# Cross-attention and experts on one core: two vectors loaded as rows, the first query's high products first, x statistics spread over the first pairs

## The reference

```python
# x (16,128,256); ctx_1024 (16,128,256); norm_w, gate_b (256,)
def xattn(h, mem):
    normed = rmsnorm(h, eps=1e-6) * norm_w
    v_pool = concat([normed, mem], axis=1)          # 256 rows per batch
    q = normed @ q_w.T;  k = v_pool @ k_w.T
    attn = softmax(where(mask, q @ k.T / 16, -inf)) # causal on the first 128, all of mem
    h_tilde = attn @ v_pool
    alpha = sigmoid(h @ gate_w.T + gate_b)
    return (1 - alpha) * h + alpha * h_tilde
x = x + xattn(layernorm(x), ctx_1024)
x = x + experts(layernorm(x), combine_weights, top_idx, W1, b1, W2, b2)   # 8 experts, 512 tokens each
```

## Time and profile before

| | us |
|---|---|
| median of 3 runs (lowest, highest) | 274.97 (274.80, 275.33) |
| the profiled execution, whole time | 275.01 |
| the profiled execution, span | 273.2 |

### The profile page before, as it was taken

One profiled execution on the slowest core, in us unless ns is written; L12 is line 12 of the kernel. 1 busy time (PEld: TensorE's weight loads), 2 busy tenths in 40 slices (PEclk: granted clock), 3 DMA queues, 4 the chain that ended last, 5 costly groups with the idle time before them and its releaser, 6 DMA issues.

```text
span 273.2 us, 5127 instructions
## 1 busy us (share of the span) xinstructions
PE 263.7 (97%) x1477; PEld 225.8 (83%) x1477; DVE 218.4 (80%) x553; ACT 188.2 (69%) x349; POOL 156.9 (57%) x152
## 2 busy tenths in 40 slices
PE   7899999999989999999999999999999999999993
PEld 3688899999876888888888888888888888888983
DVE  1899999899985779968878896796887889689453
ACT  2687899887666975786676587668657758773540
POOL 4349765565768717656456466655645656514525
PEclk9999999999999999999999999999999999999998
DMA  5986257588446945454464544645446561210211
GB/s 154 341 232 199 94 154 200 148 231 270 133 149 150 388 154 157 129 169 155 134 208 154 156 142 135 168 118 207 160 138 180 160 181 56 59 35 34 65 49 69
DMA packets 30560, 42.44 MB, mean 155 GB/s; under 512 B 5521, under 2 KB 24283, under 8 KB 30416
## 3 DMA queue, kind: packets, MB, share of 16 engines
q1 hardware_dynamic: 25120, 29.74, 35.0%
q0 software_dynamic: 4608, 12.24, 15.4%
q10 hardware_dynamic: 816, 0.26, 0.4%
HBM read 33.54 MB, written 9.24 MB: 157 GB/s over the span
## 4 chain that ended last, share of the span: by engine, by line
PE 81%; DVE 6%; issue 4%; DMA 4%; POOL 1%; ACT 1%; SPq 0%; DVEq 0%; POOLq 0%
PE bank L1423 19%; PE bank L1202 12%; PE bank L1203 12%; PE bank L1204 12%; PE bank L1424 10%; PE bank L1250 4%; PE bank L1294 3%; DMA x_all<-in_x_dram 2%; PE bank L1351 2%; DMA x_all<-token_rows,idx_all 2%; PE bank L1370 1%; PE bank L1371 1%; PE bank L1374 1%; PE bank L1318 1%; POOL out_dram L557 1%
## 5 line engine op out<-in xcount | busy, mean ns | idle before, releaser
L752 ACT ACTIVATE keysT<-bank,biasT 128x512 f32<-128x512 f32 x63 | 43.6, 692 | 55.6 <-PE bank L1204 39.3
L557 POOL DMA_INDIRECT out_dram<-h,sidx x32 | 36.7, 1146 | 40.2 <-DVE h L1094 34.8
L547 POOL DMA_INDIRECT x_all<-out_dram,idx_all x32 | 36.6, 1143 | 23.6 <-DMA out_dram<-h,sidx 16.0
L1202 PE MATMUL bank<-x_hi,w_parts 128*128 128x512 f32 (+1 forms) x114 | 45.1, 396 | 0.0
L1203 PE MATMUL bank<-x_lo,w_parts 128*128 128x512 f32 (+1 forms) x114 | 44.4, 389 | 0.0
L1204 PE MATMUL bank<-x_hi,w_parts 128*128 128x512 f32 (+1 forms) x114 | 44.1, 387 | 0.0
L1119 DVE TENSOR_TENSOR g_lo<-keysT,g_hi 128x512 fp32r<-128x512 f32 x32 | 22.1, 692 | 27.0 <-ACT g_hi L753 26.3
L543 POOL DMA_INDIRECT x_all<-token_rows,idx_all x28 | 30.7, 1095 | 18.9 <-DVE factor L1143 12.4
L1423 PE MATMUL bank<-w_parts,g_hi 128*128 128x512 f32 x112 | 40.5, 396 | 0.0
L1124 DVE TENSOR_TENSOR w_parts<-w_raw,w_parts 128x512 fp32r<-128x512 f32 x56 | 38.4, 686 | 0.0
L758 ACT CAST w_parts<-w_raw 128x512 fp32r<-128x512 f32 x56 | 34.9, 623 | 0.0
(11 more groups left out here) (187 smaller groups left out, 681.5 us busy)
## 6 DMA issues: line engine op xcount, KB each, us to landing
w_raw<-in_L_ffn_W_dram SPq DMA_DIRECT2D x32, 512.0 KB
idx_rows<-in_L_ffn_top_idx_dram SPq DMA_DIRECT2D x8, 256.0 KB, 4.1
out_dram<-x SPq DMA_DIRECT2D x8, 256.0 KB, 2.9
hn_cnat<-in_ctx_dram SPq DMA_DIRECT2D x7, 256.0 KB, 2.8
token_rows<-xn SPq DMA_DIRECT2D x7, 256.0 KB, 2.2
hn_cnat<-in_L_ffn_b_dram SPq DMA_DIRECT2D x1, 1024.0 KB
x_all<-in_x_dram SPq DMA_DIRECT2D x3, 256.0 KB, 6.8
x_all<-in_x_dram SPq DMA_DIRECT2D x1, 768.0 KB, 9.4
```

What stands on the lines that cost most here:

```text
L547: g.indirect_dma_start(accg[:, t, :], None, flat, list_of(e, t)).then_inc(acc_in[t], 16)
L557: g.indirect_dma_start(flat, idx(sidx[:, t:t + 1].bitcast(U32), 0), newrow[:, t, :], None, bounds_check=N - 1, oob_is_err=False).then_inc( ...
L752: a.activation(g32[:, f % NG, :], ps_up[f % 2][:, :], ACT.Gelu_apprx_tanh, bias=bias)
L1202: t_.matmul(dst, lhs_hi, rhs_hi, start=first, stop=False)
```

## The change

- **Vectors.** norm_w and gate_b are loaded as two rows into one partition (`vec_row`), still from ScalarE's queue behind k_w. Between `M_rows(0)` and `M_rows(1)` TensorE makes four products of a 128-wide piece of the row with a 1x1 tile `one` (set by GpSimd) and so puts the pieces in four columns of bank 6; ScalarE copies these to `norm_w_gate_bT`. All that needed norm_w by partition waits for that copy.
- **TensorE.** Eight warming products, not ten. The four spreading transposes come before hn's of pair 0. In the first query each half's four products with hnT's high part come first and its two with the low part last, and only these wait for the low part. `hn_transposes(2)` moves from before pair 0's values product to behind the list's transposes.
- **SP.** `load_ctx(0)` and `load_x(1)` change places.
- **ScalarE.** `vec_bc` is copied behind query(0) and gateT's high part; hn of pair 1 goes to VectorE; `hn_transposed(1)` moves between the two exponentials of pair 0; `hn_transposed(2)` and `normed_transposed(2)` move to the end of pair 0's body.
- **VectorE.** `x_sums` of batch 2 moves behind `hnT_low(0)`; hn of pair 1 and gateT's low part come before both masks of pair 0, h of pair 0 and `x_rms(0, 4)` behind them; statistics in groups 6-7 and 8-9 (pair 0), 10-13 (pair 1), 14-15 (pair 2), with `x_rms` for 4-9 in pair 1 and 10-15 in pair 4; the casts of lists go behind the gate logit of pair 0; `hnT_low(2)` moves to pair 1's body, where the variance of x2 also comes ahead of `hnT_low(3)`. All bodies are written out, with no loop.
- **GpSimd.** Powers and shifts follow the smaller groups, in pairs 0 to 3.

```diff
-            act.dma_start(norm_wT, norm_w.rearrange("(k p) -> p k", p=P), allow_slow_non_contiguous=True)\
-                .then_inc(nwT_in, 16)
-            act.dma_start(norm_w_gate_bT[:, 1, :], gate_b.rearrange("(k p) -> p k", p=P),
-                          allow_slow_non_contiguous=True).then_inc(gate_b_in, 16)
+            act.dma_start(vec_row[:, 0:H], norm_w.rearrange("(a h) -> a h", a=1)).then_inc(vec_in, 16)
+            act.dma_start(vec_row[:, H:2 * H], gate_b.rearrange("(a h) -> a h", a=1)).then_inc(vec_in, 16)
...
+            act.wait_ge(cols_mm, 1)
+            a.copy(norm_w_gate_bT[:, :, :].rearrange("p n k -> p (n k)"), ps_cols).then_inc(cols_rdy, 1)
...
+                    if is_first(p) and b == 0:
+                        hn_transposed(1, 1)
...
             hn_rows(0, 0)
-            x_sums(2, 3, 1)
-            dve.wait_ge(nwT_in, 16)
+            dve.wait_ge(cols_rdy, 1)
             M_low(0)
             M_low(1)
             hnT_low(0, 0)
-            x_sums(3, 4, 1)
+            x_sums(2, 4, 1)
             x_aggregates(2, 4)
             x_variances(2, 4)
             x_stats(4, 6, 2)
             x_variances(4, 6)
-            h_rows(0, 0, False)
-            x_rms(0, 4, 2)
-            x_sums(6, 8, 3)
...
+                else:
+                    dve.wait_ge(pow_rdy, 2)
+                    hn_rows(1, 1)
+                    gateT_low()
                 for b in range(2):
-                    if is_first(p) and b == 1:
-                        gateT_low()
...
+                if p == 1:
+                    hnT_low(2, 0)
...
+                    h_rows(0, 0, False)
                     hnT_low(1, 1)
+                    x_rms(0, 4, 2)
...
                 if is_first(p):
-                    x_aggregates(6, 10)
-                    x_variances(6, 10)
+                    x_stats(6, 8, 3)
+                    x_variances(6, 8)
+                    x_sums(8, 10, 3)
+                    dve.wait_ge(tok_rdy, 1)
+                    v.tensor_copy(tok_f[:, :], tok_i[:, :]).then_inc(tok_rdy, 1)
+                    dve.wait_ge(idx_in, 16)
+                    v.tensor_copy(idx_f[:, :], idx_all[:, :, :].rearrange("p t e -> p (t e)")).then_inc(idx_rdy, 1)
+                    x_aggregates(8, 10)
+                    x_variances(8, 10)
                     h_rows(1, 1, False)
-                    x_stats(10, NB, 4)
                 else:
                     stats2(p - 1, 1 - s)
-                if has_second_next(p):
+                if p == 1:
+                    aggr2(p - 1, 1 - s)
+                    x_stats(10, 14, 4)
+                    x_variances(10, 14)
+                    x_rms(4, 10, 5)
+                if has_second_next(p) and not is_first(p):
                     hnT_low(p + 2, s)
-                if is_first(p):
-                    x_variances(10, NB)
-                else:
+                if p > 1:
                     aggr2(p - 1, 1 - s)
-                    if not is_last(p):
-                        h_rows(p + 1, 1 - s)
+                if p == 2:
+                    x_stats(14, NB, 4)
+                    x_variances(14, NB)
+                if p == LAST - 3:
+                    x_rms(10, NB, 7)
+                if not is_first(p) and not is_last(p):
+                    dve.wait_ge(pow_rdy, (0, 3, 4, 5, 6, 6, 7)[p])
+                    h_rows(p + 1, 1 - s)
...
-            keep_warm(10)
+            keep_warm(8)
...
             M_rows(0)
+            pe.wait_ge(vec_in, 32)
+            pe.wait_ge(one_rdy, 1)
+            for c in range(2 * KH):
+                last = t_.matmul(ps_cols[:, c:c + 1], vec_row[:, c * P:(c + 1) * P], one[:, :], start=True, stop=True)
+            last.then_inc(cols_mm, 1)
             M_rows(1)
-            hn_transposes(0, 0)
-            pe.wait_ge(nwT_in, 16)
-            pe.wait_ge(gate_b_in, 16)
+            pe.wait_ge(cols_rdy, 1)
...
+            hn_transposes(0, 0)
             context_transposes(0, 0, 0)
             pe.wait_ge(setup_lo, 2)
-            query(0, 0)
+            pe.wait_ge(hnT_hi_rdy, 1)
+            for m in range(KH):
+                c = slice(m * P, (m + 1) * P)
+                for k in range(KH):
+                    t_.matmul(ps_q[:, m, :], M_hi[:, k, c], hnT_hi[:, 0, k, :], start=(k == 0), stop=False)
+                    t_.matmul(ps_q[:, m, :], M_lo[:, k, c], hnT_hi[:, 0, k, :], start=False, stop=False)
+                pe.wait_ge(hnT_lo_rdy, 1)
+                for k in range(KH):
+                    last = t_.matmul(ps_q[:, m, :], M_hi[:, k, c], hnT_lo[:, 0, k, :], start=False, stop=(k == KH - 1))
+            last.then_inc(q_mm, 1)
```

More of the change, by code:

```diff
@@ L76, in build_xattn_moe @@
         norm_wT = norm_w_gate_bT[:, 0, :]
+        vec_row = sb("vec_row", [1, 2 * H])
+        one = sb("one", [1, 1])
         M_hi = sb("M_hi", [P, KH, H], F32R)
@@ L438, in _ @@
             g.memset(junk[:, :], 0.0).then_inc(warm_rdy, 1)
+            g.memset(one[:, :], 1.0).then_inc(one_rdy, 1)
             g.memset(ident[:, :], 0.0).then_inc(consts, 1)
@@ L469, in _ @@
             x_powers(2, 4, 2)
-            hn_shifts(2, 4, 2)
             x_powers(4, 6, 3)
@@ L505, in attention @@
                                 h[:, s, :, :].rearrange("p b h -> p (b h)"), ALU.add).then_inc(xh_rdy, 1)
+                if p == 1:
+                    x_powers(8, 10, 5)
+                    hn_shifts(8, 10, 5)
+                if p == 2:
+                    x_powers(10, 14, 6)
+                    for b in (10, 12):
+                        hn_shifts(b, b + 2, 6)
+                if p == 3:
+                    x_powers(14, NB, 7)
+                    hn_shifts(14, NB, 7)
                 if is_last(p):
@@ L636, in hn_rows @@
             def hn_rows(p, s):
-                if not (isinstance(p, int) and p == 1):
-                    act.wait_ge(n_rdy, p - 1)
+                act.wait_ge(n_rdy, p - 1)
                 act.wait_ge(hn_rdy, 2 * p)
-                act.wait_ge(hs_rdy, p if isinstance(p, int) else 4)
+                act.wait_ge(hs_rdy, p - 1)
                 for b in range(2):
@@ L697, in attention @@
                 if is_first(p):
+                    hn_transposed(2, 0)
+                    normed_transposed(2, 0)
                     act.wait_ge(list0_mm, 1)
@@ L709, in _ @@
             normed_transposed(0, 0)
+            query(0)
+            act.wait_ge(setup_mm, 3)
+            a.copy(gateT_hi[:, :, :], ps_gate).then_inc(setup_ev, 1)
             act.wait_ge(bc_mm, 1)
             a.copy(vec_bc[:, :], banks[7][:, :]).then_inc(bc_rdy, 1)
-            query(0)
-            hn_rows(1, 1)
-            act.wait_ge(setup_mm, 3)
-            a.copy(gateT_hi[:, :, :], ps_gate).then_inc(setup_ev, 1)
             each_pair(act, attention)
@@ L981, in attention @@
                         .then_inc(late_lo_rdy, 1)
-                if is_first(p):
-                    x_rms(4, 10, 4)
-                    dve.wait_ge(x_steps, steps[0])
-                elif not is_last(p):
+                if not is_first(p) and not is_last(p):
                     shift(p - 1, 1 - s)
-                    dve.wait_ge(pow_rdy, 5)
-            each_pair(dve, attention)
+            for p in range(NPAIR):
+                attention(p, p % 2, p // 2)
             last_s = (NPAIR - 1) % 2
```

38 lines of the change are left out of this document (15 added, 23 removed).

## The result

The changed kernel takes **280.62 us** (median of four, 279.51 to 281.22) against 274.88 us (four runs of the kernel before on the same chip): ratio **1.020, 95% interval 1.018 to 1.022**. It is slower, as forecast, but by 5.6 us where 1.2 was forecast, and outside the range. The profiled execution took 279.51 us, 4.5 more than that of before.

The account below looks back on a forecast made before the run. TensorE sets the pace in mid-attention, but VectorE's order decides up to pair 3: its probability transposes come 1.25 us later (43.75 against 42.49), so 275.0 + 1.2 = 276.2 us, range 273.8 to 277.5.

Parts of the forecast that it names:

- rival (c): GpSimd's queued normed(1) takes the port between x_rms's two VectorE operations, a further 1.2 us: +2.4, 277.4 us; chance 0.10.
- hidden by the wait, if the clock stays: TensorE's start: two fewer warming products end 0.8 us before q_w, costing nothing if the clock holds.
- the price of `x_rms` beside GpSimd: VectorE in pair 0: x_rms(0,4) meets GpSimd's x_plus_h(0) and waits once, 0.8 us.
- (d): Rival, TensorE's start: eight warming products end sooner, M_rows and transposes run at 1.2 GHz: +3, 278 us; chance 0.05.
- D(1): VectorE's subtraction forming diff (line 878) on entering pair 1: forecast at 22.4 us, 1.8 earlier than before.
- D(2): The same VectorE subtraction on entering pair 2: forecast at 33.3 us, 0.9 later than before.
- D(3): The same VectorE subtraction on entering pair 3: forecast at 41.3 us; TensorE waits if later than 40.05.
- `var_eps` 0.9 of lockout: VectorE behind pair 0's residual: var_eps waits for GpSimd's back-to-back normed(2) and low part, 0.9 us.
- list transposes waiting for the cast: TensorE before the logits of pair 1: list transposes wait for VectorE's index cast, forecast at 21.0 us.
- Rival (b): Phases fall so VectorE's lockouts and waits don't meet; TensorE's chain binds: gain 1.6, 273.4 us; chance 0.25 in all.

Follow-up runs that it names:

- A: The changed kernel with ten warming products again instead of eight, nothing else: 277.70 us, ratio 1.012.
- F: A with x_rms(0, 4) moved ahead of hn of pair 1 on VectorE: 276.17 us, ratio 1.006.
- K: F with the statistics of blocks 10 to 13 moved back from pair 1 to pair 0: 275.03 us, ratio 1.002.
- I: D with the spreading transposes ahead of hn's, the first query's high products first and SP's loads exchanged: 275.50 us, ratio 1.003.
- D: The kernel before with row loads, one-column products between the halves of M_rows and ScalarE's copy, ten warming products: 274.91 us, ratio 1.002.
- C: The kernel before with eight warming products instead of ten: 274.73 us, ratio 1.002.
- E: D with eight warming products instead of ten: 276.93 us, ratio 1.010.
- B: The changed kernel, eight warming products kept, one-column products behind both halves of M_rows and hn's transposes ahead of the spreading ones: 277.60 us, ratio 1.012.
- H: The kernel before with GpSimd's powers and shifts of blocks 10 to 15 moved behind x_plus_h of pair 1: 275.14 us, ratio 1.003.
- L: K with hn's transposes ahead of the spreading ones and, in pair 1, hnT_low(3) ahead of x2's variance: 274.23 us, ratio 0.998.
- J: The kernel before with only the first query's high products put first: 274.36 us, ratio 0.999.

## Why the prediction was right or wrong

Added up by the steps of the table (2.0% in all): the clock 0.8 (after to A), rival (c) 0.6 (A to F), the place of blocks 10 to 13 0.4 (F to K), the rest 0.2.

**The start.** Forecast, and measured without the fall of the clock (A): `M_rows` 5.5 and 5.29, four products 0.9 and 0.98 start to start, hnT_low 9.75 and 9.99 (VectorE waits 0.5 for the high part), logits of pair 0 12.2 and 12.64. The packets under 512 B weren't gone (28 from 3 to 4 us and 19 from 5 to 6, against 24 and 128), but between 5 and 6 us 0.33 MB moved instead of 0.14. From the start of `M_rows` to hnT_low I had 4.25 us and A took 4.70. Most of the 0.45 is the two halves of `M_rows`: 0.86 each in my sum, 1.06 and 0.97 from start to start in A. The spreading transposes were priced right at 0.44: with them first it takes 4.70 (I), behind hn's 4.26 (D). From hnT_low to the logits I had 2.45, and it took 2.65.

**The step that failed first** is "hidden by the wait, if the clock stays". I priced its failure about right (+3; measured 1.9 at hnT_low and 2.9 in the medians) but gave it 0.05. What I took for evidence, a clock of 1.00, was of another stretch, and the start's own column would have read 1.00 too. Two products fewer cost 0.2% (C), the one-column products 0.2% (D), both 1.0% (E); and with eight warming products the loss goes when the one-column products stand behind `M_rows` (B). So the loss is shown to hang on both. The mechanism is shown for one trace, after's, where the fall follows the one-column products; E's trace lost its time otherwise, by a late rise. A change that takes work out of the warming and puts work of one column in the middle of the first real product should have had more.

**The step that failed second** is the price of `x_rms` beside GpSimd: 0.8 forecast, 1.75 measured (0.86 and 1.21 against 0.16 each). Rival (c) named it, +2.4 in all, with a chance of 0.10. GpSimd had both operations queued, and with nothing between them on its side the second starts before VectorE's next small operation can; so (c) was the thing to expect, and the forecast's single wait the exception. A, which has this step and not the fall, measured 277.70 for (c)'s 277.4. In the Trainium skill, "SBUF — State Buffer", section Who interferes with whom, the first to issue has the ports for its whole instruction; the rows at 18.81 and 19.70 agree, twice in a row. Its sentence that a VectorE instruction with two SBUF inputs contends with any GpSimd one that reads SBUF is wider than the rows: beside the power of 2.57 us from 24.07 in H, `rms` took 0.17.

**The range failed by its make.** (c) and (d) were listed as alternatives, but nothing makes them exclude each other, and both came: 277.4 and 3 more is 280.4, against 280.62 measured. That it is so close is luck, since what two of the four executions lost is not known.

**What held.** After D(1) the sum is right to 0.1 us per pair: D(1) to D(2) 10.9 forecast, 11.00 measured; D(2) to D(3) 8.0 and 8.10; `var_eps` 0.9 of lockout, 0.75 measured; D(3) to the transposes 2.44 and 2.39; list transposes waiting for the cast (1.63, though near 24 and not 21); TensorE idle 1.68 ahead of the probability transposes of pair 2 and 0.16 ahead of pair 3's. D(1) itself came 2.9 later than 22.4: 1.9 of it the clock, the rest `x_rms`. `h` lost 0.5 beside `normed`, not 0.85. F, which has neither the fall nor `x_rms`'s loss, gives 276.17 for the 276.2 of the forecast, and pair 3's transposes at 43.83 for 43.75. That is closer than the steps deserve: F's forecast would lack the 0.8 of `x_rms`, and its profiled execution (276.83, its longest) had a start 0.8 later than A's. Rival (b), that the phases fall better, was wrong for the change and half right for the idea: L reaches 0.14%, not the 1.6 us of (b), since TensorE's chain is 0.8 ahead at the logits of pair 2 (29.84 against 30.66) and not 1.6.

**Left open.** Why the clock rose late in E, F and J and fell in after, no trace here shows, nor what the two longest executions of after (281.1, 281.2), the two of E (278.0, 278.1) and the four of C (275.8 to 276.2) lost: none of them has the mean clock of a fall. Whether eight warming products make a late rise more frequent or only dearer can't be told from one trace each. Nor was it tried whether one-column products cost the clock as such, or only as time in which nothing longer runs.

## What to carry to other kernels

Before trimming what keeps TensorE busy ahead of its first product, look at the products right behind it: compare the duration of one and the same product from its first to its second use, as the clock column reads 1.00 over the cold start in every trace here. And look at more than one execution, for the clock rose between 4.0 and 7.3 us. A VectorE operation on a few numbers can cost as much as the GpSimd operation beside it, once for each one that GpSimd has queued; put it where GpSimd waits, raises powers, or has nothing. Work spread "more evenly" is worth its place, not its amount: K moved the same work by one pair for 1.1 us. And rivals that don't exclude each other must be added up in the range.

## What was not expected of the hardware

- TensorE's clock fell from 1.00 to 0.50 right behind eight records of one-column products that took 1.05 us, with TensorE 100% busy by the page from 6 to 8 us. No execution of A (ten warming products) or B (the same products 0.7 us later) has a mean clock low enough for such a fall.
- The granted clock reads 1.00 before its first recorded change, though TensorE runs at half speed: 0.43 us between warming products of 512 columns until the rise, 0.22 after it (A); with ten warming products the rise came at 4.0 to 4.9 us in most traces and near 6.8 in one (F).
- A one-column float32 product is two records of 0.12 us each start to start (8 in 0.98), against 0.25 for 256 columns (8 in 1.99).
- While two 1 KB vectors came in 4-byte pieces, the whole core moved 0.14 MB from 5 to 6 us; with rows, 0.33. It was worth 0.5 us to one load and nothing to the time (D).
- VectorE's operations on 128x4 and 128x2 wait out a whole GpSimd operation on 128x512 (1.21 and 0.92 us), not a power on GpSimd (0.16 and 0.17).
